# An fp32 transformer block on one core: attention tiles in four slots of a head pair, P scaled and k rotated on GpSimd

## The reference, cut to what matters

```python
h = shift_token(x)                       # second half of the channels from the row before
q, k, v = jnp.split(h @ wqkv, 3, axis=-1)          # 8 heads of 64
q = l2norm(q) * qs;  k = l2norm(k) * ksc
q, k = rotary_xpos(q, k)                 # rotation with a position-dependent scale
o = local_attention(q, k, v)             # windows of 256: own block and the one before, masked to 256 back
x = x + o @ wo
h = layernorm(shift_token(x)) * lg + lb
a, g = jnp.split(h @ w1 + b1, 2, axis=-1)
x = x + (a * gelu(g)) @ w2 + b2
```

## Time and profile before

| quantity | value |
|---|---|
| median of 3 runs | 3651.58 us (3651.21 to 3654.27) |
| profiled execution | 3654.35 us |
| its span, first to last instruction | 3652.6 us |
| busy in the span | PE 94%, DVE 56%, ACT 42%, POOL 17% |
| mean granted TensorE clock | 0.977 |

### The profile page before, as it was taken

One profiled execution on the slowest core, in us unless ns is written; L12 is line 12 of the kernel. 1 busy time (PEld: TensorE's weight loads), 2 busy tenths in 40 slices (PEclk: granted clock), 3 DMA queues, 4 the chain that ended last, 5 costly groups with the idle time before them and its releaser, 6 DMA issues. The chain is left out here.

```text
span 3652.6 us, 57089 instructions
## 1 busy us (share of the span) xinstructions
PE 3439.7 (94%) x19728; PEld 2775.2 (76%) x19728; DVE 2047.0 (56%) x4772; ACT 1550.6 (42%) x3549; POOL 628.9 (17%) x1352
## 2 busy tenths in 40 slices
PE   5995999999998899999996899999999799999999
PEld 5884777777777688888784677777777578888887
DVE  2554777777777533333333677777777643333333
ACT  1113777777676211111111667676767311111111
POOL 0003222323233500000001323232323600000000
PEclk9997999999999899999997999999999899999999
DMA  3223111011112311111113011111111521111110
GB/s 111 70 76 115 59 50 59 27 59 50 59 50 82 110 55 58 58 58 58 58 58 126 19 59 50 59 50 59 50 46 40 157 72 58 58 58 58 58 54 34
DMA packets 172722, 232.31 MB, mean 64 GB/s; under 512 B 25448, under 2 KB 99304, under 8 KB 172184
## 3 DMA queue, kind: packets, MB, share of 16 engines
q1 hardware_dynamic: 155544, 211.88, 17.6%
q10 hardware_dynamic: 16896, 16.78, 1.4%
HBM read 134.22 MB, written 60.83 MB: 53 GB/s over the span
## 5 line engine op out<-in xcount | busy, mean ns | idle before, releaser
L295 PE MATMUL bank<-f_hT_hi,f_w_hi 128*128 128x512 f32 (+1 forms) x1408 | 559.8, 398 | 14.9 <-ACT f_hT_hi L948 14.9
L297 PE MATMUL bank<-f_hT_hi,f_w_lo 128*128 128x512 f32 (+1 forms) x1408 | 557.4, 396 | 0.0
L296 PE MATMUL bank<-f_hT_lo,f_w_hi 128*128 128x512 f32 (+1 forms) x1408 | 556.7, 395 | 0.0
L964 ACT ACTIVATE f_gate<-bank,f_b 128x512 f32<-128x512 f32 (+1 forms) x176 | 121.2, 689 | 1001.5 <-PE bank L297 1001.5
L1295 DVE SCALAR_TENSOR_TENSOR f_uraw<-bank,f_b,f_gate 128x512 f32<-128x512 f32 (+1 forms) x176 | 132.1, 751 | 717.4 <-ACT f_gate L964 717.2
L1174 DVE TENSOR_TENSOR a_PT_lo<-bank,a_PT_hi 128x384 fp32r<-128x384 f32 x512 | 284.3, 555 | 214.2 <-ACT a_PT_hi L900 207.5
L889 ACT ACTIVATE a_P<-a_S,a_bias 128x384 f32<-128x384 f32 x512 | 311.1, 608 | 170.8 <-DVE a_bias L1162 170.8
L295 PE MATMUL bank<-a_PT_hi,a_V_hi 128*64 128x128 f32 x1536 | 335.8, 247 | 0.0
L894 ACT ACTIVATE a_P<-a_P,a_inv 128x384 f32<-128x384 f32 x512 | 308.1, 613 | 31.5 <-DVE a_inv L1170 14.7
L295 PEld LDWEIGHTS bank<-f_hT_hi,f_w_hi 128*128 128x128 f32 (+1 forms) x1408 | 260.7, 185 | 79.7 <-ACT f_hT_hi L948 15.6
L297 PEld LDWEIGHTS bank<-f_hT_hi,f_w_lo 128*128 128x128 f32 (+1 forms) x1408 | 261.2, 186 | 67.6
(11 more groups left out here) (165 smaller groups left out, 7520.9 us busy)
## 6 DMA issues: line engine op xcount, KB each, us to landing
a_h<-x_layer_in SPq DMA_DIRECT2D x144, 128.0 KB, 2.4
a_res<-x_layer_in SPq DMA_DIRECT2D x66, 256.0 KB, 2.8
x_after_attention<-out_tiles SPq DMA_DIRECT2D x64, 256.0 KB, 2.0
f_h<-x_after_attention ACTq DMA_DIRECT2D x32, 512.0 KB, 4.6
f_res<-x_after_attention SPq DMA_DIRECT2D x64, 256.0 KB, 3.5
f_x<-in_x SPq DMA_DIRECT2D x64, 256.0 KB, 3.2
x_layer_in<-f_res SPq DMA_DIRECT2D x64, 256.0 KB, 2.9
out<-f_res SPq DMA_DIRECT2D x64, 256.0 KB, 3.0
```

Of the source, the lines that this page charges most:

```text
L295: pe.matmul(dst, w[0], m[0], start=start, stop=False)
L296: pe.matmul(dst, w[0], m[1], start=False, stop=False)
L297: return pe.matmul(dst, w[1], m[0], start=False, stop=stop)
L964: act.activation(f_gate[0:ROWS[m], m % 2, :], bank[pair_of(u, m) + 1][0:ROWS[m], :], ACT.Gelu, bias=f_b1[0:ROWS[m], 1, m:m + 1]).then_inc( ...
```

## The change

An attention tile is now four slots (A to D) of a head pair, and all engines follow steps `t` that mix four tiles:

- The scores of a pair are issued together, one head on partitions 0 to 63 and one on 64 to 127, and one slot ahead of their use. P has four buffers (three before). A pair's six transposes go to two neighbouring banks and are split by one ACT and one DVE instruction of 768 elements per partition; the outputs of all heads gather in two banks and are split at the tile's end, two instructions each.
- P is normalized by POOL (`normalize`: two multiplications per pair), no more by ACT.
- k is copied out of PSUM by ACT (`k_copy`) and rotated by POOL (`rotate_k`, three instructions); DVE keeps `k_norm`. Steps of `rotate_q` are interleaved with normalize.
- Each projection is one run of 12 matmuls in one shared bank (`work`), all h, q and k transposes use another (`turn`). q and k of tile t+2 are projected in step t, v of t+1, the output of t-1.
- No tile beyond the last is prepared. Masks are indexed directly, POOL's mask copies go. Weights are staged in the order k, q, v, o.

```diff
-        bank = [... psum_tensor(f"bank{i}", [P, 512], F32)) for i in range(8)]
+        pt_banks = ctx.enter_context(nc.psum_tensor("bank23", [P, 2, 512], F32))
...
-            a_P = s("a_P", [P, 3, WIN * P])
+            a_P = s("a_P", [P, 4, WIN * P])
...
 PE
+                def scores(x, i):
...
+                    pe.wait_ge(a_S_masked, START + (G + x) * H + 2 * i)
+                    for odd in range(2):
+                        r = slice(odd * HD, odd * HD + HD)
+                        three_passes(pe, bank[odd][:, 0:WIN * P], [a_QT[n][r, i, :] for n in range(2)],
+                                     [a_KT[n][r, i, j * P:(j + WIN) * P] for n in range(2)], True, True)\
+                            .then_inc(a_S_mm, 1)
+                def p_T(x, i):
+                    pe.wait_ge(a_P_set, START + (G + x) * H + 2 * i + 2)
+                    pe.wait_ge(a_PT_lo, START + (G + x) * PAIRS + i)
...
+                for t in STEPS:
+                    A: scores(t, 1)      pv(t - 1, 3)  p_T(t, 0)            v_project(t + 1)
+                    B: scores(t, 2)      pv(t, 0)      p_T(t, 1)  k_T(t+1)  project_out(t - 1)
+                    C: scores(t, 3)      pv(t, 1)      p_T(t, 2)  q_T(t+1)  k_project(t + 2)
+                    D: scores(t + 1, 0)  pv(t, 2)      p_T(t, 3)  h_T(t+3)  q_project(t + 2)
 ACT, in the order of its queue
+                    square(0, t + 1)  q_copy(t + 1)  o_hi(t - 1)
+                    p_T(t, 0)  exp(t, 2)  exp(t, 3)  value(t + 1)
+                    exp(t, 4)  p_T(t, 1)  k_T(t + 1)
+                    exp(t, 5)  exp(t, 6)  p_T(t, 2)  q_T(t + 1)
+                    exp(t, 7)  square(1, t + 2)  k_copy(t + 2)
+                    exp(t + 1, 0)  p_T(t, 3)  h_T(t + 3)  exp(t + 1, 1)
 DVE
+                    sums(0, t + 1)  mask_max(t, 2)  mask_max(t, 3)  o_lo(t - 1)
+                    p_T(t, 0)  k_norm(t + 1)  inverse(t, 1)  value(t + 1)
+                    mask_max(t, 4)  mask_max(t, 5)  p_T(t, 1)  k_T(t + 1)  inverse(t, 2)  result(t - 1)
+                    mask_max(t, 6)  mask_max(t, 7)  p_T(t, 2)  q_T(t + 1)  inverse(t, 3)
+                    sums(1, t + 2)  mask_max(t + 1, 0)  mask_max(t + 1, 1)
+                    p_T(t, 3)  h_T(t + 3)  inverse(t + 1, 0)
 POOL
+                def rotate_k(x):
+                    pool.wait_ge(a_k_copied, START + G + x + 1)
+                    pool.wait_ge(a_KT_mm, START + G + x)
+                    pool.tensor_tensor(halves(a_tmp[:]), halves(a_kraw[:])[:, :, ::-1, :], table(x, 3), ALU.mult)
+                    pool.tensor_tensor(halves(a_krot[:]), halves(a_kraw[:]), table(x, 2), ALU.mult)
+                    pool.wait_ge(a_krot_step, START + 2 * (G + x) + 2)
+                    pool.tensor_tensor(a_krot[:], a_krot[:], a_tmp[:], ALU.add).then_inc(a_k_rotated, 1)
+                def normalize(x, i):
+                    pool.wait_ge(a_inv_set, START + (G + x) * PAIRS + i + 1)
+                    for h in (2 * i, 2 * i + 1):
+                        pool.tensor_scalar(a_P[:, h % 4, :], a_P[:, h % 4, :], a_inv[:, x % 2, h:h + 1], None, ALU.mult)\
+                            .then_inc(a_P_set, 1)
+                    norms(t + 1)  rotate_q(t + 1, (0,))  normalize(t, 1)  rotate_q(t + 1, (1,))
+                    normalize(t, 2)  normalize(t, 3)  rotate_k(t + 2)  normalize(t + 1, 0)
 SP
+                    if here(t) and t % QUAD == 2 and t // QUAD < BLOCKS - 1:
+                        carry(t // QUAD)
+                    store(t - 1)  load_res(t + 1)  load_h(t + 3 + QUAD)
```

More of the change, by code:

```diff
@@ new lines, in project @@
+                def project(which, x, done):
+                    if x == 0:
+                        pe.wait_ge(a_w_hi, START + 4 * l + W_ORDER.index(which) + 1)
+                        pe.wait_ge(a_w_lo, START + 4 * l + W_ORDER.index(which) + 1)
+                    for k in range(KT_):
+                        mm = three_passes(pe, work[:], [a_hT[i][:, x % 2, k, :] for i in range(2)],
+                                          [a_w[which][i][:, k, :] for i in range(2)], k == 0, k == KT_ - 1)
+                    mm.then_inc(done, 1)
@@ new lines, in attention @@
+                for t in STEPS:
+                    if here(t):
+                        scores(t, 1)
+                    if here(t - 1):
+                        pv(t - 1, 3)
+                    if here(t):
+                        p_T(t, 0)
+                    if here(t + 1):
+                        v_project(t + 1)
+                    if here(t):
+                        scores(t, 2)
+                        pv(t, 0)
+                        p_T(t, 1)
+                    if here(t + 1):
+                        k_T(t + 1)
+                    if here(t - 1):
+                        project_out(t - 1)
+                    if here(t):
+                        scores(t, 3)
+                        pv(t, 1)
+                        p_T(t, 2)
+                    if here(t + 1):
+                        q_T(t + 1)
+                    if here(t + 2):
+                        k_project(t + 2)
+                    if here(t + 1):
+                        scores(t + 1, 0)
+                    if here(t):
+                        pv(t, 2)
+                        p_T(t, 3)
+                    if here(t + 3):
+                        h_T(t + 3)
+                    if here(t + 2):
+                        q_project(t + 2)
@@ L1083, in attention, with sums @@
             def attention(l):
[L1084 to L1087 removed]
+                G = l * TILES
+                quarters = lambda ap: ap.rearrange("p (k n) -> p k n", k=4)
+                turn, work = bank[6], bank[7]
+                def sums(which, x):
+                    dve.wait_ge((a_q_squared, a_k_squared)[which], START + G + x + 1)
+                    dve.wait_ge(a_norms_set, START + G + x)
```

828 lines of the change are left out of this document (390 added, 438 removed).

## The result

The changed kernel takes 3866.61 us (3865.35 to 3871.46, four runs), against 3651.8 us for the kernel before on the same chip: a ratio of 1.0589, 95% interval 1.0571 to 1.0608. It is 5.9% slower. The forecast was 3601 us, with a range of 3517 to 3673, so both the sign and the size were wrong. The profiled execution has a span of 3863.6 us.

What follows compares the result with a forecast made beforehand. Attention was taken as PE bound at 26.24 us a tile; afterwards the norm chain and POOL's scaling would set 25.6, saving 25.4 us a layer, 51 in two layers: 3601 us, range 3517 to 3673.

Steps and rivals of the forecast that it cites:

- norms set: End of the norm chain from ACT's square through POOL's small steps, 6.56 us after slot A begins.
- the collision: POOL's q rotation step (1.28 us) and DVE's k_norm (0.69) exclude each other, taken in series in each tile.
- the price of POOL's multiplication: One scaling of 128x384 of P on POOL: 0.55 us, 1.1 a pair, bounded by 0.50 and 0.96.
- Rival 4: POOL's multiplication takes 0.96 us: tile 26.4, 3649 us, no change; at 1.1 each, 26.7 and 3667; chance 0.20.
- ready at A + 1.0: Pair 0's scaling on POOL, ready 1.0 us into slot A, needed at 1.98, so costed at nothing.
- Rival 3: PE's stall of 2.4 us per tile lowers the granted clock, costing 1.9 us: tile 27.5, 3715 us; chance 0.10.
- The forecast's own stall of 2.4 us: PE's wait in each tile ahead of pair 1's transposes, until POOL has scaled P.
- PE's sum: PE's own work over the four slots of a tile: 23.26 us, 2.98 less if nothing else binds.
- Rival 2: PE stays the bound in attention: tile 23.3 us, 94 us less a layer, 3463 us; chance 0.08.
- The drain: End of each attention layer, from the start of step 30 to the last result: 47.5 us, between 38 and 60.
- the fill: Start of a layer's attention, from q's weights to the first full step: step 0 begins at 341.2 us.
- The formula 385.8 + 30 T: End of a layer's attention from fill, drain and tile time T: 1153.8 us at T = 25.6, against 1179.2 before.

Runs made afterwards that it cites:

- experiment 6: Changed kernel with POOL's multiplication written as a product of two tensors, the reciprocal broadcast along the columns: 3722.23 us, ratio 1.0186 to the kernel before.
- experiment 4: Changed kernel plus thirty transposes of the identity on PE ahead of the wait for pair 1: 3781.81 us, ratio 1.0351 to the kernel before.
- experiment 1: Changed kernel with POOL multiplying only 16 of the 384 columns of P, the rest unscaled: 3591.48 us, ratio 0.983 to the kernel before.
- experiment 3: Changed kernel, multiplication still on POOL, with inverse(t,1) ahead of k_norm on DVE and normalize(t,1) ahead of POOL's first q rotation step: 3744.42 us, ratio 1.0252.
- experiment 2: Changed kernel with P's multiplication back on ACT, all else as changed: 3536.43 us, ratio 0.9676 to the kernel before.
- experiment 7: Changed kernel with k's three rotation steps moved from POOL to DVE ahead of k_norm, multiplication still on POOL: 3952.7 us, ratio 1.0816.
- experiment 5: experiment 2 with inverse(t,1) ahead of k_norm on DVE: 3449.2 us, ratio 0.9438 to the kernel before.
- experiment 10: experiment 5 with k's rotation moved from POOL to DVE ahead of k_norm: 3499.71 us, ratio 0.9583 to the kernel before.
- experiment 8: experiment 5 with P's multiplication on DVE right behind each inverse instead of on ACT: 3451.54 us, ratio 0.9446 to the kernel before.

## Why the prediction was wrong

Take the tile whose slot A begins at A = 693.68 (ACT's square starts 0.1 after it, at 693.79); the next begins at 722.71, 29.03 us later. The prediction's steps, one by one:

| step | forecast | measured | difference |
|---|---|---|---|
| norms set | A + 6.56 | A + 7.34 | +0.78 |
| from there to normalize(t,1), with the collision and the inverse | 2.24 | 1.83 | -0.41 |
| normalize, a pair | 1.1 | 2.47 | +1.37 |
| hand-over | 0.0 | 0.06 | +0.06 |
| p_T(t,1) starts | A + 9.9 | A + 11.70 | +1.80 |
| rest of slot B | 4.0 | 5.39 | +1.39 |
| slots C and D | 11.84 | 11.94 | +0.10 |
| tile | 25.7 | 29.0 | +3.3 |

- **The step that failed is the price of POOL's multiplication.** The prediction put it "nearest to the copy" at 0.55 and closed the bound at 0.96. It is 1.24. The bound was drawn from the wrong rows: neither a copy nor a product of two tensors says what a product with a scalar costs on POOL, and experiment 6 shows that the product with two tensors (0.83) is cheaper than the one with one (1.24). The 0.96 did hold for the form that it was drawn from. Rival 4, which had 1.1 as a second value, gave it the right mechanism and 3667 us; even there the sum lacked the two things below.
- **The price is paid twice.** normalize(t,0) was costed at nothing: "ready at A + 1.0". At 2.46 us a pair it ends at 695.95, A + 2.27, and the first norm step, due at A + 1.6, starts behind it at 696.04. This is the +0.78 of the table's first row. The prediction said that each covered edit costs what exceeds its slack, but worked out this slack only against PE and not against what is queued behind it on POOL. With both pairs, 2.1 of the table's 3.3 us follow from the one price.
- **Rival 3, the clock, was true.** It had 0.10. Behind each stall of 3.8 us the granted clock falls to the lower of its two levels, 1.2 GHz, and part of the transposes and of the output projection runs at that level. The rival's price was 1.9 us; measured were 1.39 in the table and 1.44 by experiment 4, and between neighbouring tiles with and without the fall 1.6 (26.4 and 24.8, experiment 1) and 1.9 (28.25 and 26.37, experiment 3). It and rival 4 were treated as exclusive, but the longer stall of rival 4 brings the fall of rival 3 with it. The forecast's own stall of 2.4 us was not run, but its neighbours were: 2.67 us lost the clock in every tile (experiment 6), 2.5 us in every other (experiment 3), 1.7 us in some (experiment 1), 1.2 us in none (experiment 2). An estimate from these: a fall of 1.9 us in every other tile on top of T = 25.6 is 26.55, 3601 + 57 = 3658 us, no gain. So the forecast was unsafe even with the multiplication at its price of 0.55.
- **The collision was right in kind and overpriced.** k_norm and the rotation step start 0.05 us apart. DVE wins in all 64 tiles: k_norm keeps its 0.69, the rotation takes 1.77 instead of 1.27, and the inverse isn't delayed by POOL. The cost is 0.50, where 0.69 and the inverse in series were taken; the two ran side by side for 0.64, so POOL did not lose the whole of it. The Trainium skill, page "SBUF — State Buffer", section "Who interferes with whom", says that a DVE instruction with two SBUF inputs contends with a GpSimd instruction that reads SBUF; the trace agrees, here and in experiment 7 (0.22 to 0.54 to 0.65).
- **PE's sum was right.** 23.26 forecast, 22.83 with all waits gone (experiment 5), no PE idle left. P·V was 4.6 instead of 5.04, the small transposes 0.36 instead of 0.42, P's transposes 2.6 instead of 2.3. Rival 2 (3463 us, "PE stays the bound") is thus the fastest version to within 14 us, but only with the multiplication on another engine and the inverse moved.
- **The drain was too short, the fill was right.** The formula 385.8 + 30 T with T = 29.36 gives 1266.6, measured 1283.5. Step 0 starts at 341.39, where 341.2 was forecast. Step 30 starts at 1222.52, 3.4 later than the formula has it, and from there to the last store are 61.0 us, put at 47.5 with an upper bound of 60. With the scaling on ACT (experiment 5) this drain is still 53.1 us (1026.28 to 1079.4), so 5.6 us were missing from the forecast's own sum and 7.9 come with POOL's scaling.

Together: 30 x (29.36 - 25.6) = 113 and 16.9 for fill and drain together are 130 us a layer, 3601 + 260 = 3861, against 3866.6 measured. By the runs, the change without POOL's scaling gains 117 us (experiment 2 against the kernel before on its chip), and P's scaling on POOL loses 330. What k's rotation on POOL has in the 117 us isn't separated; in the version without any PE wait it is worth 50 us (experiment 10).

No run puts POOL's multiplication alone into the kernel before; whether its 1.24 us would have been hidden there, with heads of 3.3 us (26.24 / 8) and scores two heads ahead, wasn't tried.

The Trainium skill, page "GPSIMD Engine Reference", section "Engine selection", says of elementwise work that GpSimd is about half as fast as VectorE with two inputs and that with one input it is roughly at line rate. The first half agrees with this case: the rotation steps of 128x512 took 1.28 us on POOL and 0.69 on DVE. The second half doesn't hold here: multiplied by a scalar, 128x384 took 1.24 us on POOL and 0.42 on DVE (experiment 8), three times as long, and the measurement decides. The advice of the Trainium skill on that page, to give elementwise work to VectorE, was right for P's scaling, and not for k's rotation, which lost 50 us in the place on DVE that experiment 10 gave it.

## What to carry to other kernels

Where an operation moves to an engine on which the trace has no row of just that operation, its price is open on the upper side too: bound it by more than the nearest-looking row, and add it at each place where it stands in that engine's queue, with what is queued behind it. A stall that comes once in every tile costs more than its length, since the clock can fall behind it; price the two together. And the order of two small steps (a reciprocal of 0.16 us ahead of a k_norm of 0.69 us that waits for the norms) was worth 87 us once the multiplication was off POOL, so after regrouping look at what the shortest instruction on the chain stands behind.

## What the hardware showed that wasn't expected

- POOL on 128x384 fp32: times a scalar through a pointer 1.24 us, times a constant 1.17, times a broadcast tensor 0.83, copy 0.50 at its fastest. On 128x16 the pointer form takes 0.33. ACT does the same scaling in 0.61, DVE in 0.42.
- With one long stall of PE in each tile, the granted clock fell to the lower level from 456 to 913 us behind 16 of 16 stalls of 3.8 us, 17 of 17 of 2.67 us (experiment 6), 9 of 17 of 2.5 us (experiment 3), 6 of 18 of 1.7 us (experiment 1) and none of 19 of 1.2 us (experiment 2). Thirty dummy transposes in the stall kept it at 1.00 and were worth 85 us.
- When DVE's and POOL's instructions with SBUF inputs started 0.05 us apart, DVE's ran undisturbed in all 64 cases (691 to 695 ns) and POOL's was stretched (1765 to 1800 ns).
